# Graph attention: five units in eight, in place of four, transposed in blocks by VectorE and carried through memory, with a third block buffer

## The reference, cut to what matters

```python
# for each of the two layers, for each of the eight heads
q, k, v = x @ Wq[l] + bq[l], x @ Wk[l], x @ Wv[l]     # 1024 x 64 per head
a = q @ k.T * 64 ** -0.5                              # 1024 x 1024 per head
p = exp(a masked and weighted by the edges, less the row's maximum)
out = (p @ v) / p.sum(axis=-1)                        # per head
x = x + out @ Wo[l] + bo[l]; batch norm; feed-forward; batch norm
```

## Time and profile before

| | |
|---|---|
| median of 3 runs | 1045.06 us (1043.06 to 1047.96) |
| profiled execution, its own time | 1045.83 us |
| its span in the trace | 1043.8 us |
| TensorE matmul busy | 962.8 us, 92% of the span |
| VectorE busy | 632.3 us, 61% |
| ScalarE busy | 491.8 us, 47% |
| GpSimd busy | 246.1 us, 24% |
| DMA queue of SyncE | 93.11 MB, 28.3% of 16 engines' span |
| mean granted TensorE clock | 0.983 |

### The profile page before, as it was taken

How to read it: one execution, slowest core, us unless ns; L and a number is a source line. 1 busy time by engine, 2 the same in 40 slices (tenths; PEclk the granted TensorE clock), 3 DMA queues, 4 the chain that set the end, 5 groups by cost and what they waited for, 6 DMA issues and landing times.

```text
span 1043.8 us, 15195 instructions
## 1 busy us (share of the span) xinstructions
PE 962.8 (92%) x5346; PEld 676.4 (65%) x5346; DVE 632.3 (61%) x1087; ACT 491.8 (47%) x766; POOL 246.1 (24%) x137
## 2 busy tenths in 40 slices
PE   6999999999989999989999998999899999989915
PEld 2835545888777787777777676744667776767413
DVE  4775476468776235447767764534477667745395
ACT  1664444555624214137666664113476666641054
POOL 2000000699922051500000047011000000480400
PEclk9999999999999999999999999999999999999978
DMA  9201100000200301235666671101056665811102
GB/s 327 67 0 41 41 1 21 1 1 1 81 1 1 115 6 41 81 130 188 183 186 182 187 246 33 45 36 40 11 181 184 189 183 178 261 28 35 69 0 81
DMA packets 58848, 96.14 MB, mean 92 GB/s; under 512 B 8284, under 2 KB 38172, under 8 KB 58270
## 3 DMA queue, kind: packets, MB, share of 16 engines
q1 hardware_dynamic: 55454, 93.11, 28.3%
q10 hardware_dynamic: 3328, 2.15, 0.7%
HBM read 59.58 MB, written 33.55 MB: 89 GB/s over the span
## 4 chain that ended last, share of the span: by engine, by line
PE 70%; DVE 9%; POOL 7%; issue 6%; ACT 3%; DMA 2%; SPq 1%; DVEq 0%; ACTq 0%; POOLq 0%
PE slots L1785 62%; PE slots L1852 8%; POOL MASK L696 2%; DMA PT<-blocks 1%; POOL MASK L690 1%; POOL KR L695 1%; POOL X L727 1%; DMA W<-in_wkT 1%; SPq L594 1%; POOL PT L687 1%; DVE XT L1514 1%; ACT X L1100 1%; DVE Q1L L1502 0%; DVE X L1669 0%; DVE XT L1535 0%
## 5 line engine op out<-in xcount | busy, mean ns | idle before, releaser
L1785 PE MATMUL slots<-PT,XN 128*64 128x256 f32 x1024 | 117.6, 382 | 4.1 <-DMA PT<-blocks 4.1
L1574 DVE CUSTOM_DVE_ANT_0 SM<-slots,MASK 128x1024 f32<-128x1024 f32 x64 | 75.7, 1220 | 72.1 <-PE slots L1785 72.1
L1785 PE MATMUL slots<-KS,QS 64*128 64x512 f32 x768 | 105.6, 406 | 7.7 <-DVE nm L1574 3.5
L1785 PEld LDWEIGHTS slots<-PT,XN 128*64 128x64 f32 x1024 | 73.4, 137 | 45.3 <-issue 13.5
L751 POOL TENSOR_TENSOR QS<-QF,QS 128x512 fp32r<-128x512 f32 x16 | 20.6, 1289 | 324.6 <-ACT QS L1031 324.6
L1785 PEld LDWEIGHTS slots<-KS,QS 64*128 64x128 f32 x768 | 70.8, 185 | 27.8 <-issue 9.7
L1015 ACT ACTIVATE SM<-SM,nm 128x1024 f32<-128x1024 f32 x64 | 73.3, 1146 | 23.8 <-DVE nm L1574 23.2
L795 ACT ACTIVATE PT<-slots 128x1024 f32<-128x1024 f32 x68 | 69.3, 1019 | 31.3 <-PE slots L1852 26.3
L1785 PE MATMUL slots<-PT 128*128 128x512 bf16 (+3 forms) x408 | 80.3, 368 | 2.3 <-ACT PT L795 1.2
L1015 ACT ACTIVATE PT<-PT,nm 128x1024 f32<-128x1024 f32 x64 | 73.3, 1145 | 17.0 <-DVE nm L1574 16.5
L1574 DVE CUSTOM_DVE_ANT_0 PT<-slots,MASK 128x1024 f32<-128x1024 f32 x64 | 75.2, 1211 | 4.2 <-PE slots L1785 4.0
(11 more groups left out here) (396 smaller groups left out, 2173.7 us busy)
## 6 DMA issues: line engine op xcount, KB each, us to landing
blocks<-FL SPq DMA_DIRECT2D x56, 512.0 KB, 3.2
PT<-blocks SPq DMA_DIRECT2D x224, 128.0 KB, 3.4
X<-in_x SPq DMA_DIRECT2D x4, 512.0 KB, 11.5
W<-in_wout SPq DMA_DIRECT2D x2, 1024.0 KB, 6.5
W<-in_gq SPq DMA_DIRECT2D x2, 1024.0 KB, 5.2
W<-in_gk SPq DMA_DIRECT2D x2, 1024.0 KB, 5.3
spill<-X SPq DMA_DIRECT2D x4, 512.0 KB, 2.6
SXR<-XTR SPq DMA_DIRECT2D x1, 2048.0 KB, 8.4
```

Source lines behind the costliest of these rows:

```text
L1574: nc.vector.tensor_tensor_reduce(out=SMs[n % SMB], in0=src, in1=MASK[:, unit(n)[2], :], scale=-1.0, scalar=-0.1 * NO_EDGE, op0=ALU.add, op ...
L1785: return nc.tensor.matmul(o_, lhsT, rhs, start=start, stop=stop)
```

## The change

Of every eight units one more is flipped, the unit with n % 8 == 2, and FL gets a third buffer. In a layer 35 units are flipped in place of 28, seven more: the units 2, 10, 18, 26, 34, 42 and 50. Each stands right before a unit that was flipped already, so that the steps 2, 10, 18, ... flip both their units.

```diff
-FLIPS = [n for n in range(UNITS - 8) if n % 2 == 1]
-FLIP_BUFFERS = 2
+FLIPS = [n for n in range(UNITS - 8) if n % 2 == 1 or n % 8 == 2]
+FLIP_BUFFERS = 3
```

## The result

The changed kernel takes 1076.12 us (median of 4 runs, 1072.77 to 1076.84), the kernel before beside it 1046.12 (4 runs, 1043.06 to 1047.96). The ratio is 1.0281, with a 95% interval of 1.0251 to 1.0311: slower, by 30 us where 16 were forecast, and 2 us above the top of the range. The profiled execution of the change has a span of 1074.2 us and a mean granted clock of 0.968; before it was 1043.8 and 0.983.

The account below looks back on a forecast made before the run. TensorE, gapless inside the second attention, was taken as the bound, with fetch landings setting six tight groups. Tight groups lose 14.0 us, others gain 1.2, the clock costs 3.4: 1045.06 + 16.2 = 1061 us, range 1047 to 1074.

Parts of the forecast that it names:

- aggregates 2 to 8: Even groups with slack: each gains 0.97 us or slack less delay, if smaller; taken as 0.6 us gained a layer.
- aggregate 12, its fetch: Tight group at aggregate 12, a tie before: its later fetch costs 2.3 us a layer, between groups 0 and 10.
- clock behind aggregate 10: Behind aggregate 10's wait in both layers: granted clock 0.50 for 3.35 us, losing 1.7 us each, 3.4 in all.
- The gain: TensorE loses fourteen turns of 0.97 us each: 13.6 us, the whole gain the change can have.
- VectorE: Fourteen more flips of 1.24 us; evictions end 1.17 us later, almost a tie with TensorE's need; taken as 0.
- SyncE's order: With T the issue of the step's first sending, the sending of 4g+3 goes out at T + 2.75, behind a fetch.
- The landing of that sending: Sending of 4g+3 lands 3.6 us after issue, so its fetch starts at T + 6.5, 2.1 to 2.6 us late.
- slack: Time the fetch has to spare before its aggregate: 2.1 us in group 2, 3.0 in 4, 1.6 in 6; 8 like 4.
- The tight groups: Aggregates 0, 10 and 12, started by their landings: lose 2.6, 2.1 and 2.3 us, 7.0 a layer, 14.0 in all.
- The clock: TensorE idles 3.1 us and more at aggregate 10, then runs at 1.2 GHz: 3.4 us over both layers.
- Rival 3: Burst fills the DMA engines, clock falls at every tight place: delays 3.4 to 3.9 us, 1086 us; chance 0.10.
- Rival 1: Queue is cheap: issuing is short beside the transfer, only VectorE's 1.17 us delays the fetch; 1045 us; 0.13 with what is near.

## Why the forecast had the sign and not the size

The shifts of the aggregates, in us a layer, by the forecast's own terms (the first layer's from the rows above, without the 1.2 us that lie ahead of its first trip, in code that the change doesn't touch):

| term | forecast | layer 1 | layer 2 |
|---|---|---|---|
| aggregate 0 | 2.6 | 3.6 | 2.9 |
| aggregates 2 to 8 | −0.6 | 2.9 | 2.9 |
| aggregate 10 | 2.1 | 2.8 | 3.3 |
| aggregate 12, its fetch | 2.3 | 3.0 | 3.2 |
| clock behind aggregate 10 | 1.7 | 2.9 | 2.4 |
| clock behind aggregate 12 | 0 | 2.4 | 1.7 |
| end of the layer | 0 | −2.7 | −2.6 |
| sum | 8.1 | 14.9 | 13.7 |

Worked out for the first layer: aggregate 0 487.48 − 482.70 = 4.8, less 1.2; aggregate 8 585.61 − 577.93 = 7.7, so 2.9 more; aggregate 10 610.60 − 600.13 = 10.5; aggregate 12 638.84 − 622.48 = 16.4, of which 6.58 − 3.67 = 2.9 are the slow aggregate 10; aggregate 13 652.58 − 633.78 = 18.8; aggregate 15 670.08 − 653.96 = 16.1. The second layer is read in the same way, and the terms are rounded. With the 1.2 us ahead and 0.6 behind the attentions, this is the 30.4 us between the spans.

- **The gain** of 0.97 us a turn: right. Aggregates 1, 3, 5, 7 and 9 show it one by one, and so do the kernels with the trips elsewhere.
- **VectorE**, taken at nothing: right but for one place. Ahead of aggregate 0 the scores wait 2.38 us for VectorE's `nm`, but there the landing sets the start anyway. In the groups 2 to 8 of the first layer no score waits for it.
- **SyncE's order** (sending of 4g+3 at T + 2.75): right to 0.1 us, and shown to matter by ScalarE's sendings (12 us); the trips elsewhere (31 us) show it together with the load. The list as a whole was a little too short: SyncE is through at T + 6.5 and not at 5.9, since the fetch of 4g+2 takes 2.58 us to issue in the mean, where 2.27 were taken.
- **The landing of that sending, "I take 3.6"**: this is the step that failed. Measured are 4.47. It came from one sending behind a fetch in a group with fewer transfers and a median of 3.2. The sample was a fair one for the kernel before: the twenty sendings of the units 5, 9, ... 41 there, issued 0.2 to 1.3 us behind a fetch, land in 3.7 us in the mean and 5.0 at most. What it missed is the fuller burst. Of the 0.8 us by which the fetch starts later than forecast, this landing is about 0.65 and SyncE's longer list 0.15 (an estimate: with 3.6 in place of each group's landing, the fetches would start at T + 6.65 in the mean). From there on the fetch takes as long as forecast, within 0.1. Together the blocks are there 3.15 us later than before, where 2.1 to 2.6 were forecast. That is a small error for a group, but it falls on the far side of the slack: with 1.6 to 3.0 us of slack the groups 2 to 8 were to gain 0.6 us a layer and lost 2.9. The rows to read were the DMA share in the burst, and the longest of rows 7, 5.0 us, which the forecast kept for its bounds only. The half bytes show it from the other side: 2.6 us less in the trip, and the layer gains. But one landing is not the whole of it: with both sendings ahead of the fetches it was 3.0 to 3.2 us in most groups, and the blocks came no earlier. What stays is the load of six transfers in 13 us; how its time divides among them is open.
- **The tight groups** 0, 10 and 12: the right ones, each forecast 0.3 to 1.2 us too small.
- **The clock**: the right mechanism, at half its size. The fall lasted 6.8 us in place of 3.4, and it came with aggregate 12 as well (6.8 us in the first layer, 3.4 in the second). The last line of the table is partly the clock too: the fall that the kernel before has at the end of the layer is absent from the change, which is worth 1.7 of the 2.7; the other microsecond stays open.
- **Rival 3** (a full burst, and clock falls) named what happened; it had the delay at 3.4 to 3.9 us, over the 3.15 measured, and the clock's six falls at 10 us, where the rows give 2.9 + 2.4 + 2.4 + 1.7 = 9.4 for four of them (the two ahead of aggregate 0 cost nothing there, since the landing sets its start), less the fall at the end of each layer that went away. Halfway between it and the forecast, at 1074, is where the range ended.
- **Rival 1** and the rule beside it: the Trainium skill ("DMA: Bandwidth & Descriptors", Issuing engines are not separate DMA queues) has it that the issue time saved by another issuing engine is usually small. Here it saves 12 of 1076 us in the change, and about 4 of 1047, with the late load that alone brings nothing, in the kernel before. By that rule the second fits and the first doesn't.
- The Trainium skill's clock rule ("TensorE: Matmul & The Clock Gate", HAM oscillation): waits on DMAs make the bursts of matmuls behind them slow. The change's trace agrees for the waits of 3.9 to 4.9 us; behind those of 1.1 to 1.9 in the groups 2 to 8 the aggregates keep their 3.67 us.

## What to carry to other kernels

A transfer's latency is to be read from a stretch as full as the one it will stand in: take the DMA share of the burst and not of the stage, and set the longest landing of the old trace, not the median, against the slack of each group. Where work moves to a path that is a chain of trips with little slack, a late trip loses the whole gain and not a part of it; put the extra trips where their landing is wanted last (one unit's number was worth 31 us here), and take their issues off the queue on which the urgent one waits. And a wait of 3.9 to 4.9 us on TensorE cost another 1.7 to 2.9 us behind it.

## What the runs showed of the chip

- A sending of 512 KB lands in 2.9 to 3.2 us in a lull. In a burst of six transfers (DMA share 0.89) it lands in 3.9 to 5.3 us right behind a fetch, and in 3.0 to 3.2 in 11 of 14 groups ahead of the fetches. Behind a weight load of 1 MB it took 10.86. With 256 KB in the same burst it is 2.96 behind a fetch, and the last 64 KB of a fetch land in 2.01.
- Eight DMA issues in a row cost SyncE about 4.3 us in most groups and 5.53 at most, and a sending right behind a fetch is issued in 0.38 where a lone one takes 0.34.
- A granted clock of 0.50 came for 3.4 or for 6.8 us at the end of the waits of 3.9 to 4.9 us, and not where TensorE had 16 matmuls (3.93 us) to do ahead of the same place. Behind the change's waits of under 2 us in mid-layer it stayed at 1.00; in another kernel a wait of 2.14 us was followed by a fall and one of 2.27 us wasn't.
